# One block from the second layer to the attention, batch norm coefficients by halves, and other fills ahead of the convolution

## What is computed

```python
# second layer (graph convolution with two batch norms over all rows)
agg = einsum('nm,bmd->bnd', A_hat, features)
h = relu(batchnorm(agg @ W1.T + b1, g1, be1))      # 128 -> 256 features
out = batchnorm(h @ W2.T + b2, g2, be2)            # 256 -> 128 features
# third layer: two graph convolutions, then LSTMs over windows of 1 to 4 nodes
h = relu(einsum('ts,bsh->bth', adj, x @ Wg0 + bg0))
h = relu(einsum('ts,bsh->bth', adj, h @ Wg1 + bg1))
for p in range(1, 5): h = lstm_last_states(windows_of(h, p))
```

## Time and profile before

| | |
|---|---|
| median of three runs | 1221.98 us (1221.71 to 1222.08) |
| the profiled execution | 1222.5 us |
| its span from the first to the last instruction | 1220.8 us |
| PE busy | 1186.0 us (97%) |
| DVE busy | 980.9 us (80%) |
| ACT busy | 901.9 us (74%) |
| POOL busy | 428.2 us (35%) |
| granted PE clock, mean | 0.996 |

### The profile page before, as it was taken

How to read it: one execution, slowest core, us unless ns; L and a number is a source line. 1 busy time by engine, 2 the same in 40 slices (tenths; PEclk the granted TensorE clock), 3 DMA queues, 4 the chain that set the end, 5 groups by cost and what they waited for, 6 DMA issues and landing times.

```text
span 1220.8 us, 22403 instructions
## 1 busy us (share of the span) xinstructions
PE 1186.0 (97%) x7262; PEld 1023.4 (84%) x7262; DVE 980.9 (80%) x2005; ACT 901.9 (74%) x1733; POOL 428.2 (35%) x794
## 2 busy tenths in 40 slices
PE   8999999989999998999999999999999999989998
PEld 8999988843688886689888988898898899978997
DVE  6888859977688876888788878887887899987774
ACT  5766779978578876877787768776776688875554
POOL 5878748700276430000000000000000377757764
PEclk9999999999999999999999999999999999999999
DMA  8000000000311100000000000000300030001112
GB/s 322 1 2 2 1 1 1 0 1 0 112 62 69 69 35 1 1 1 1 1 1 1 2 1 1 1 1 1 138 1 1 2 139 2 2 1 51 72 70 87
DMA packets 14924, 38.23 MB, mean 31 GB/s; under 512 B 1904, under 2 KB 3952, under 8 KB 13808
## 3 DMA queue, kind: packets, MB, share of 16 engines
q1 hardware_dynamic: 14000, 36.60, 7.9%
q10 hardware_dynamic: 832, 0.46, 0.1%
HBM read 20.27 MB, written 16.78 MB: 30 GB/s over the span
## 4 chain that ended last, share of the span: by engine, by line
PE 53%; DVE 5%; ACT 2%; issue 1%; POOL 1%; POOLq 0%; DVEq 0%; ACTq 0%
PE psum L1197 7%; PE psum L1198 7%; PE psum L1199 7%; PE psum L1216 5%; PE psum L1212 4%; PE psum L1213 4%; PE psum L1484 2%; PE psum L1736 2%; PE psum L1701 2%; PE psum L1490 2%; PE psum L1711 2%; ACT gates L1235 2%; PE psum L1503 1%; PE psum L1504 1%; PE psum L1722 1%; PE psum L1366 1%
## 5 line engine op out<-in xcount | busy, mean ns | idle before, releaser
L1235 ACT ACTIVATE gates<-psum,lstm_bias 128x512 f32<-128x512 f32 (+1 forms) x504 | 302.2, 637 | 101.8 <-PE psum L1216 88.3
L143 POOL TENSOR_TENSOR l2r_sum<-l2r_st 128x8 f32<-128x8 f32 x16 | 5.2, 323 | 518.0 <-DVE l2r_st L116 517.7
L175 ACT ACTIVATE l_h<-X,nmr,rstd 128x128 f32<-128x128 f32 (+1 forms) x392 | 160.6, 484 | 14.6 <-POOLq L169 14.6
L1198 PE MATMUL psum<-lstm_node_hi,Wih_lo 128*128 128x512 f32 (+1 forms) x408 | 148.3, 363 | 0.0
L1197 PE MATMUL psum<-lstm_node_hi,Wih_hi 128*128 128x512 f32 (+1 forms) x408 | 148.1, 363 | 0.0
L1199 PE MATMUL psum<-lstm_node_lo,Wih_hi 128*128 128x512 f32 (+1 forms) x408 | 148.0, 363 | 0.0
L1212 PE MATMUL psum<-lstm_hid_hi,Whh_hi 128*128 128x512 f32 (+1 forms) x288 | 104.7, 363 | 3.9 <-DVE lstm_hid_hi L1295 3.8
L1216 PE MATMUL psum<-lstm_hid_lo,Whh_hi 128*128 128x512 f32 (+1 forms) x288 | 108.0, 375 | 0.0
L1213 PE MATMUL psum<-lstm_hid_hi,Whh_lo 128*128 128x512 f32 (+1 forms) x288 | 103.6, 360 | 0.0
L1240 ACT ACTIVATE gates<-lstm_cell 128x512 f32<-128x512 f32 (+1 forms) x144 | 83.7, 581 | 21.0 <-DVE lstm_cell L1282 20.6
L1197 PEld LDWEIGHTS psum<-lstm_node_hi,Wih_hi 128*128 128x128 f32 x408 | 77.3, 190 | 10.9 <-ACT gates L1235 0.3
(11 more groups left out here) (277 smaller groups left out, 3456.9 us busy)
## 6 DMA issues: line engine op xcount, KB each, us to landing
x_spill<-X SPq DMA_DIRECT2D x32, 256.0 KB, 2.0
X<-x_spill SPq DMA_DIRECT2D x2, 4096.0 KB, 12.3
out<-X SPq DMA_DIRECT2D x32, 256.0 KB, 2.0
X<-in_x SPq DMA_DIRECT2D x6, 1024.0 KB, 15.3
X<-in_x SPq DMA_DIRECT2D x3, 512.0 KB, 8.7
w_raw<-in_WihT SPq DMA_DIRECT2D x1, 1024.0 KB, 5.6
w_raw<-in_WhhT SPq DMA_DIRECT2D x1, 1024.0 KB, 7.8
X<-in_x SPq DMA_DIRECT2D x2, 256.0 KB, 3.2
```

The costliest lines, as they stand in the source:

```text
L175: last = act.activation(h[:, j, :], k.X[:, bass.ds(b0, TB), :][:, j, :], ACT.Relu, bias=k.nmr[:, bass.ds(b0, TB)][:, j:j + 1], scale=k.rst ...
L1198: pe.matmul(out, lo, x_high, start=False, stop=False)
L1235: act.activation(gate_of(it, g), k.bank[4 * s + g][:, 0:it.N], ACT.Tanh if g == GATE_G else ACT.Sigmoid, bias=k.lstm_bias[:, it.p - 1, g:g ...
```

## The change

The four stages behind the first layer are no blocks of their own any more. Their functions return the engines' programs, and one block runs them one behind the other. Three barriers go. Waits on counted semaphores take their place: `stats_done` (all statistics are taken) ahead of each `bn_aggr`, `h2_ready` on SP ahead of the load of the LSTM weights (whose place held `h2` and `Y1`), `w_split` on PE and `spilled` on DVE ahead of the LSTM. The clear of the semaphores moves to the end of the first layer, keeps those that the second layer goes on with, and so takes two ranges.

```diff
-    def recycle_semaphores(self):
+    def recycle_semaphores(self, kept):
-        self.nc.clear_and_free_semaphores(list(self.sems))
+        self.nc.clear_and_free_semaphores([sem for sem in self.sems if sem not in kept])
         self.nc.all_engine_barrier()
-        self.sems = ()
+        self.sems = tuple(kept)
...
             stage_first(k, c, d, e)
+        k.recycle_semaphores([k.hidden_h_done, e.l3_in] + k.l0_ln.semaphores())
...
-            k.recycle_semaphores()
...
+        with nc.Block() as block:
...
+            @block.tensor
+            def _(pe):
+                hidden.on_tensor(pe)
+                gcn_out.on_tensor(pe)
+                conv.on_tensor(pe)
+                states.on_tensor(pe)
```

```diff
     def on_vector(dve):
+        dve.wait_ge(*stats_done)
+        for c in range(halves):
+            dve.bn_aggr(mv[:, c, :], bn6[:, c, :, :]).then_inc(aggregated, 1)
+            dve.wait_ge(aggregated, c + 1)
+            dve.tensor_scalar(mv[:, c, 1:2], mv[:, c, 1:2], EPS, None, ALU.add).then_inc(shifted, 1)
         for c in range(halves):
-            last = dve.bn_aggr(mv[:, c, :], bn6[:, c, :, :])
-        last.then_inc(aggregated, 1)
-        dve.wait_ge(aggregated, 1)
-        dve.tensor_scalar(mv[:, :, 1], mv[:, :, 1], EPS, None, ALU.add).then_inc(shifted, 1)
...
+            dve.wait_ge(powed, c + 1)
+            dve.tensor_tensor(a, k.cols[:, c_gamma + c:c_gamma + c + 1], power, ALU.mult).then_inc(scaled, 1)
```

In out each half of `h2` has a semaphore count of its own, and PE waits for it ahead of the matmul that reads it. The first tile of either buffer is written out ahead of ACT's loop. The fills around it change:

```diff
+                if isinstance(i, int) and i == s == 0:
+                    act.wait_ge(coef_ready, c + 1)
+                act.activation(h2[s][:, c, :], Y[c][:, bass.ds((i * S + s) * TW, TW)], ACT.Relu,
+                               bias=coef[:, c, 1:2], scale=coef[:, c, 0:1]).then_inc(h2_ready[s], 1)
...
-            stay_awake(pe, k, k.bank[7], 16)
+        stay_awake(pe, k, k.bank[7], 44)
             with pe.Fori(0, n_it) as i:
                 for s in range(S):
-                    pe.wait_ge(h2_ready[s], i + 1)
+                pe.wait_ge(h2_ready[s], 2 * i + 1)
                     pe.wait_ge(O_stored[s], i + 1)
                     pe.matmul(psO[s][:, :], k.W2T[:, 0, :], h2[s][:, 0, :], start=True, stop=False)
+                pe.wait_ge(h2_ready[s], 2 * i + 2)
                     pe.matmul(psO[s][:, :], k.W2T[:, 1, :], h2[s][:, 1, :], start=False, stop=True).then_inc(O_ready[s], 1)
-            stay_awake(pe, k, k.bank[7], 6)
+        stay_awake(pe, k, k.bank[7], 12)
```

In the convolution POOL takes two turns of coefficients ahead of the first split, and the fills stand elsewhere:

```diff
-    FILL = {-4: 8, -3: 6, -2: 10, -1: 10, 0: 10, 1: 8, 2: 6, 3: 4}
+    FILL = {-2: 6, -1: 6, 0: 30, 1: 2}
...
+        AHEAD = 2
+        for i in range(AHEAD):
+            res.coefficients(pool, i)
             for n, W in enumerate((k.Wih, k.Whh)):
                 pool.wait_ge(w_in[n], 16)
                 with pool.Fori(4 * n, 4 * n + 4) as i:
-                    res.coefficients(pool, i)
+                res.coefficients(pool, i + AHEAD)
...
-            stay_awake(pe, k, k.bank[7], 8)
+        stay_awake(pe, k, k.bank[7], 22)
```

More of the change, by code:

```diff
@@ L682, in batchnorm_coefficients, with on_pool, step @@
-def batchnorm_coefficients(k, ctx, name, bn6, halves, c_gamma, c_beta, coef):
+    def on_pool(pool):
+        def step(i, s):
+            t = i * S + s + 1
+            if there(t) and parted(t):
+                pool.wait_ge(Z_done, t - S + 1)
+                x, mine = k.X[:, bass.ds(t * TB, TB), :], h[(s + 1) % S][:, MINE:, :]
+                for j in range(MINE, TB):
+                    last = pool.tensor_scalar(h[(s + 1) % S][:, j, :], x[:, j, :], k.rstd[:, bass.ds(t * TB, TB)][:, j:j + 1],
+                                              k.nmr[:, bass.ds(t * TB, TB)][:, j:j + 1], ALU.mult, ALU.add)
+                last.then_inc(scaled, 1)
+                pool.wait_ge(scaled, t - PARTED + 1)
+                pool.sem_inc(tally, 1)
+                pool.tensor_scalar(mine, mine, 0.0, 0.0, ALU.max, ALU.add).then_inc(part_done, 1)
+        k.l0_ln.coefficients(pool, n_it // L0_TURNS - 1)
+        for t in range(tiles):
+            step(t // S, t % S)
@@ new lines, in on_tensor @@
+    def on_tensor(pe):
+        for s in range(S):
+            pe.sem_inc(O_ready[s], 1)
+        stay_awake(pe, k, k.bank[7], 44)
+        with pe.Fori(0, n_it) as i:
+            for s in range(S):
+                pe.wait_ge(h2_ready[s], 2 * i + 1)
+                pe.wait_ge(O_stored[s], i + 1)
+                pe.matmul(psO[s][:, :], k.W2T[:, 0, :], h2[s][:, 0, :], start=True, stop=False)
+                pe.wait_ge(h2_ready[s], 2 * i + 2)
+                pe.matmul(psO[s][:, :], k.W2T[:, 1, :], h2[s][:, 1, :], start=False, stop=True).then_inc(O_ready[s], 1)
+        stay_awake(pe, k, k.bank[7], 12)
@@ L1014 @@
+    programs = Programs(on_sync=on_sync, on_pool=on_pool, on_scalar=on_scalar, on_tensor=on_tensor, on_vector=on_vector)
+    programs.spilled, programs.w_split, programs.H_done = (spilled, tiles * 16), (w_split, 8), (H_done, tiles)
+    return programs
 GATE_I, GATE_F, GATE_G, GATE_O = range(4)
@@ new lines, in on_sync @@
+    def on_sync(sp):
+        for s in range(S):
+            free = max(it.n for it in items if it.slot == s and it.last and it.half == 0)
+            sp.wait_ge(computed[s], free + 1)
+        head = k.B // 2
+        sp.dma_start(k.X[:, 0:head, :], k.x_spill[:, 0:head, :]).then_inc(x_head, 16)
+        for s in range(S):
+            sp.wait_ge(computed[s], ends[s].n + 1)
+        sp.dma_start(k.X[:, head:, :], k.x_spill[:, head:, :]).then_inc(x_tail, 16)
+        sp.wait_ge(x_head, 16)
+        sp.wait_ge(x_tail, 16)
+        at.on_sync(sp)
```

825 lines of the change are left out of this document (405 added, 420 removed).

## The result

| | before | after |
|---|---|---|
| median, 20 runs each | 1221.83 us (1220.37 to 1223.06) | 1219.90 us (1217.72 to 1221.74) |
| ratio, 95% interval | | 0.9983 [0.9977, 0.9990] |
| the profiled execution, span | 1222.5 us, 1220.8 us | 1221.55 us, 1219.6 us |
| granted PE clock in it, mean | 0.996 | 0.994 |

The changed kernel is 1.9 us faster, with an interval of 1.2 to 2.8 us, so the difference is real but small: by the bound that the prediction set (0.2%) it is no change. 1220.9 us was forecast. One execution of experiment 12 took 1677.95 us at a mean granted clock of 0.654, a slow state that no ratio here counts.

The account below looks back on a forecast made before the run. PE, busy 97% with work and fills, was taken to bound the kernel. Terms of 1.2 - 0.85 - 1.1 - 0.3 = -1.05 us took the profiled 1222.5 to 1221.4 us, 1220.9 us as median; range 1217.8 to 1224.0 us.

Parts of the forecast that it names:

- Price of a fill: Fills on PE: 0.1125 us a record, 0.225 us a matmul of two records, and 0.15 us overlapped at the end.
- the rival of shorter fills in a long row: Rival, chance 0.03: a fill record takes 0.08 us in a long row; 5.7 us more gain, 1215.2 us.
- Step 1: End of the first layer: two clears and a second barrier make it later by 1.2 us, bounds 0.8 and 1.9 us.
- Step 2: Hidden to out: 56 fills in one row end behind the sooner data; out's first product later by 3.0 us.
- with at most 35 fills they would show: Hidden to out: with no more fills than that, the halves of the coefficients, some 0.5 us sooner, would show.
- Step 3: Loop of out: PE waits for half a tile, 1.72 us a tile against 1.841; shorter by 3.9 us.
- The rival in which the turn of DVE's loop costs it its spare time: Rival, chance 0.13: DVE holds the loop of out at its old rate; 1224.7 us, 0.2% slower.
- Step 4: Out to the convolution's steady part: 1.1 us earlier, bounds 2.1 us earlier and no gain; fills set the first product.
- It doesn't bind: Convolution: POOL's work behind its two early turns, busy for 53.43 of 94 us before, doesn't hold PE up.
- Step 5: Convolution to LSTM: the 0.29 us barrier goes, 0.3 us earlier.
- The clock: Rival at the LSTM, chance 0.12: less idle time on PE, both half-clock stretches go, 2.8 us more gain, 1218.1 us.
- It didn't fall behind the first layer: Rival, chance 0.06: PE's longer idle time behind the first layer lowers its clock, 1.4 us lost, 1222.3 us.

Follow-up runs that it names:

- experiment 12: The changed kernel with batch norm coefficients computed as before the change, without halves, all its fills kept: 1219.49 us, 0.9985.
- Experiment 6: The changed kernel with one more all-engine barrier behind the clears at the end of the first layer: run once, 1219.05 us.
- experiment 2: The changed kernel with 22 fills in place of 44 ahead of out's first product: 1216.65 us, 0.9963.
- experiment 5: The kernel before with one edit, PE waits for each half of h2 in the loop of out: 1217.79 us, 0.9967.
- experiment 7: The combination: changed kernel with fewer fills ahead of out and convolution, nine ahead of the LSTM, and DVE's bank-free signal sent earlier: 1210.45 us, 0.9907.
- experiment 8: The kernel of experiment 7 with batch norm coefficients computed as before the change, without halves: 1211.52 us, 0.9913.
- experiment 11: The changed kernel with POOL's two early turns of layer norm coefficients taken back, all its fills kept: 1220.35 us, 0.9989.
- experiment 9: The kernel of experiment 7 with POOL's two early turns of layer norm coefficients taken back: 1212.99 us, 0.9929.
- experiment 1: The changed kernel with the old numbers of fills, those of the kernel before, put back: 1216.5 us, 0.9959.
- experiment 3: The changed kernel with 10 fills in place of 22 ahead of the convolution's first transposes, and a shorter fill list: 1215.15 us, 0.9949.
- experiment 4: The changed kernel with nine fills added ahead of the LSTM, where PE was idle: 1219.22 us, 0.9979.

## Why the prediction was right

The dates of PE in the changed kernel, each against before and without some 0.17 us by which this execution was already later ahead of the clears (its fills behind the first layer start at 167.72 us, before at 167.56):

| step | forecast | measured |
|---|---|---|
| 1, end of the first layer | +1.2 us | +1.03 |
| 2, first product of out | +3.0 | +2.94 |
| 3, loop of out | -3.9 | -3.97 |
| 4, out to steady convolution | -1.1 | -1.41 |
| 5, convolution to LSTM | -0.3 | -0.31 |
| sum | -1.05 | -1.72, and -1.55 with the 0.17 us |
| median | -1.1 | -1.93 (1.2 to 2.8) |

**Price of a fill: right.** 112 records in one row took 12.50 us up to the product behind them, 0.112 us each, so the rival of shorter fills in a long row is dead. The Trainium skill's figure of about 81 ns for a matmul of 128 columns (TensorE: Matmul & The Clock Gate, Back-to-back issue gap) is not met by any of these rows. The prediction set it against a record; the matmul, of two records, took 0.223 us.

**Step 1: right, 0.17 us too large.** I had allowed a second clear up to the price of the first. Experiment 6 has two clears at 0.70 us where one was 0.77.

**Step 2: right in its date, wrong in an aside.** The fills set the first product, and the coefficients' gain is hidden (experiment 12). But "with at most 35 fills they would show" fails: experiment 2 had 34, and PE waited for DVE's signal behind the projections. I had read ACT as PE's last wait and did not ask what was late next. This is DVE in the kernel before:

```profile
256.41 0.23 DVE L784 COPY W1T<-Wqv 128x128 f32<-128x128 f32 x1
```

If the signal follows the start of this copy by 0.08 us, as in experiments 2 and 5, it came at about 256.5 us (an estimate), only 0.1 us ahead of PE's start at 256.59. With the signal moved the halves show, 0.8 us (experiments 7 and 8).

**Step 3: right.** Experiment 5 isolates it on the kernel before: 1.72 us a tile. The rival in which the turn of DVE's loop costs it its spare time is dead: its stores start at 264.49, 266.21 and 267.92 us, 1.72 apart across a turn.

**Step 4: right in kind, 0.3 us too small.** It is the largest miss of the five, and made of small ones. The first product came at 20.12 us (20.3 forecast), because the work and the fills ahead of it took 0.18 us less than reckoned. Tile 3 came 10.57 us behind it (10.7 forecast). Of these 10.57 us 9.67 are work and the two fills, so the waits cost 0.90 us where I had 1.0. The row at 340.53 shows only 0.44 us of idle time, since it is counted from the end of the record before, while the records overlap each other in a full row. "It doesn't bind", said of POOL, is true for the work behind its early turns. The turns themselves are worth 1.0 us here (experiment 11) and 2.5 us once the fills are cut.

**Step 5: right**, 0.31 us.

**The clock: neither forecast nor rival holds as written.** It didn't fall behind the first layer. At the LSTM the profiled execution has a longer half-clock stretch than before, yet two of the 20 runs of the changed kernel had a mean clock of 0.999 and a span of 1216.0 and 1216.1 us, which with the 1.7 us around the span is close to the rival's 1218.1 us. Both happen in the same program. So the rival was no separate outcome but the lower end of a spread, and a forecast of one number needed that spread around it. The spread is not the same in both kernels: none of the 55 runs of the kernel before that stand beside the experiments shows a mean clock above 0.997 or a span below 1218.7 us, and 5 of the changed kernel's 20 show 0.998 or 0.999. So the rival came true in part, and why the changed kernel keeps its clock more often stays open.

So the difference between 1.05 and the median's 1.93 us is, as far as dates show it, step 4 (0.31), step 1 (0.17) and steps 2 and 3 (0.06 and 0.07). The rest, 0.3 us, is smaller than the interval. The clock may hold it: among the runs with a mean clock of 0.997, the kernel before has spans of 1218.7 to 1219.4 us (14 runs) and the changed one 1217.3 to 1218.0 us (5 runs), 1.4 us apart by their medians, which is nearer to the dates than to 1.93. That is a comparison of a few runs and no proof.

Where did the change's own gain go? Its loop is worth 4.2 us alone (experiment 5), its early turns and halves up to 2.5 and 0.8 us. Its fills ahead of out took 3.4 us back (3.1 by the dates), and the seam behind the first layer 1.0 us.

## What to carry to other kernels

A fill is paid whenever it ends behind the data, and it hides every improvement of that data: after any change that brings data sooner, set the number of fills again from the date of the last wait, in a profile that has too few. When a wait is removed, look for the signals that the same engine awaits in the same place and where in their engine's program they are sent. Here a "bank is free" stood behind 1.9 us of unrelated work, and cost nothing until the neighbour became early. If a matmul accumulates over parts that arrive one after the other, let it wait for each part.

## What the runs showed that I had not expected

**The spread of runs of one program goes with the mean granted clock.** The changed kernel's 20 runs: spans of 1216.0 to 1216.6 us at a clock of 0.998 and 0.999, 1217.3 to 1218.0 at 0.997, 1218.3 to 1218.8 at 0.996, 1219.2 to 1219.6 at 0.995 and 0.994. In the kernel before the order is loose: 1218.7 to 1221.1 us at 0.996 alone. In profiles the difference stands in up to three places at which PE had idled a little, the LSTM's start, its second half-step some 30 us later, and the attention at 1060 to 1100 us. Each is mostly a stretch of some 3.5 us at half clock, which shows as 0.91 in a row of 20 us. One more such stretch costs an estimated 1.6 us: the combination's spans are 1207.1 us at 0.999 and 1208.6 to 1208.9 us at 0.997 and 0.996, of which only the first has a profile. Which of them come varies: before, experiments 2 and 11 and the changed kernel have three, experiments 5, 6, 8 and 9 two, experiments 1, 3, 4, 7 and 12 one. At the LSTM's start 7 of the 9 profiles without fills there have it, experiments 1 and 3 don't, with the same idle times of 0.78 and 2.02 us ahead of it:

```profile
461.97 0.47 PE L1218 MATMUL psum<-lstm_x_hi,Wih_hi 128*128 128x512 f32 x1 [2.02 <-DVE lstm_x_lo L1323]
```

is experiment 3, at full clock, where the changed kernel's 466.18 is at half. All five profiles with the nine fills are at full clock there. So the idle time makes the stretch possible and something else decides; what that is stays open. Fills in the other two places were not tried: the code there uses all eight PSUM banks.
